# Moving the low halves of the expert weights between VectorE's and GpSimd's queues, three more shared results kept aside, and raw weights loaded by SyncE, in a one-core transformer block

## The reference

```python
h = layernorm(x) * (1 + ca) + sa
x = x + ga * (window_attention(h) @ w_out.T)          # 16 heads, window 64
h = layernorm(x) * (1 + cb) + sb
# router: 16 experts, the best 4 for each row, with weights w
y = sum over e of coeff[:, e] * ((silu(h @ Wg[e].T) * (h @ Wu[e].T)) @ Wd[e].T)   # inner width 176
z = (silu(h @ Sg.T) * (h @ Su.T)) @ Sd.T              # shared expert, inner width 352
x = x + gb * (y + z)
```

## Time and profile before

| | |
|---|---|
| span of the profiled execution | 556.1 us |
| its time on the device | 557.91 us |
| mean granted clock of TensorE | 0.969 of full speed |
| TensorE busy | 503.4 us (91%) |
| VectorE busy | 380.4 us (68%) |
| ScalarE busy | 281.0 us (51%) |
| GpSimd busy | 301.1 us (54%) |
| chain that ended last | PE 65%, DVE 15%, issue 7%, DMA 6%, POOL 4%, ACT 2% |

### The profile page before, as it was taken

How to read it: one execution, slowest core, us unless ns; L and a number is a source line. 1 busy time by engine, 2 the same in 40 slices (tenths; PEclk the granted TensorE clock), 3 DMA queues, 4 the chain that set the end, 5 groups by cost and what they waited for, 6 DMA issues and landing times.

```text
span 556.1 us, 11906 instructions
## 1 busy us (share of the span) xinstructions
PE 503.4 (91%) x3457; PEld 462.8 (83%) x3457; DVE 380.4 (68%) x1051; ACT 281.0 (51%) x735; POOL 301.1 (54%) x261
## 2 busy tenths in 40 slices
PE   2699999999999998999878787899999999999966
PEld 0589998999898898989655576789999999999956
DVE  6769952545768678686777668977677677777443
ACT  2358764464445545444463446455556555564311
POOL 6546611010225464354657539987766676677671
PEclk9999999999899999999777899999999999999979
DMA  7556996689678485642367447557777886776586
GB/s 195 150 164 215 259 304 193 176 216 221 179 235 252 145 242 162 195 126 75 123 231 237 149 126 163 88 104 133 130 122 129 198 129 128 129 130 111 103 260 151
DMA packets 72499, 94.23 MB, mean 169 GB/s; under 512 B 9339, under 2 KB 61882, under 8 KB 72118
## 3 DMA queue, kind: packets, MB, share of 16 engines
q1 hardware_dynamic: 53368, 60.35, 40.2%
q0 software_dynamic: 16384, 27.32, 23.9%
q10 hardware_dynamic: 2686, 5.81, 3.5%
HBM read 57.27 MB, written 41.88 MB: 178 GB/s over the span
## 4 chain that ended last, share of the span: by engine, by line
PE 65%; DVE 15%; issue 7%; DMA 6%; POOL 4%; ACT 2%; SPq 0%; DVEq 0%; POOLq 0%; ACTq 0%
PE GU_e L108 12%; PE YP_e L108 11%; PE O L1402 8%; PE QB L108 5%; PE VB L108 4%; PE TB L1392 3%; PE SB L1380 3%; PE HT_e L1982 3%; PE XT_e L1972 3%; POOL acc L1846 2%; PE TB L1390 2%; DMA acc<-h,ids_st 2%; PE SB L1377 2%; DVE lo L194 2%; PE Y L1419 2%
## 5 line engine op out<-in xcount | busy, mean ns | idle before, releaser
L1846 POOL DMA_INDIRECT acc<-h,ids_st x59 | 93.4, 1583 | 38.4 <-DMA acc<-h,ids_st 15.0
L143 POOL DMA_INDIRECT xs_scr<-h,slot_u x64 | 63.0, 984 | 62.0 <-PE TB L1392 25.3
L108 PE MATMUL GU_e<-gu_hi,xT 128*128 x316 | 82.6, 343 | 1.5 <-DVE xT L1873 0.8
L108 PE MATMUL YP_e<-dn_hi,aT 88*128 x316 | 67.6, 306 | 6.0 <-DVE aT L1878 6.0
L1772 ACT ACTIVATE aT<-HT_e 88x256 fp32r<-88x256 f32 (+1 forms) x89 | 34.9, 394 | 69.1 <-PE HT_e L1982 69.1
L949 ACT ACTIVATE prob<-TB 128x512 f32<-128x512 f32 x64 | 38.2, 597 | 58.2 <-PE TB L1392 57.4
L1402 PE MATMUL O<-raw,prob 128*128 128x99 f32 x512 | 67.1, 278 | 0.0
L1402 PEld LDWEIGHTS O<-raw,prob 128*128 128x128 f32 x512 | 62.4, 194 | 0.1
L1885 DVE TENSOR_TENSOR h_act<-GU_e,g_act 128x176 f32<-128x176 f32 (+1 forms) x89 | 32.0, 360 | 43.5 <-ACT g_act L1765 42.5
L108 PEld LDWEIGHTS YP_e<-dn_hi,aT 88*128 88x128 f32 x316 | 47.8, 188 | 13.0 <-issue 9.3
L108 PEld LDWEIGHTS GU_e<-gu_hi,xT 128*128 128x128 f32 x316 | 51.1, 189 | 2.1 <-issue 2.0
(11 more groups left out here) (245 smaller groups left out, 1221.9 us busy)
## 6 DMA issues: line engine op xcount, KB each, us to landing
x_st<-xs_scr SPq DMA_DIRECT2D x79, 144.0 KB
dn_hi<-k_scr SPq DMA_DIRECT2D x48, 192.0 KB, 3.9
k_scr<-raw SPq DMA_DIRECT2D x8, 768.0 KB, 6.1
dn_hi<-q_scr SPq DMA_DIRECT2D x24, 256.0 KB, 4.4
q_scr<-raw SPq DMA_DIRECT2D x8, 512.0 KB, 3.6
raw<-in_egu SPq DMA_DIRECT2D x8, 352.0 KB
raw<-in_x SPq DMA_DIRECT2D x16, 128.0 KB, 3.9
x_res<-in_x SPq DMA_DIRECT2D x32, 64.0 KB, 3.3
```

The source lines that it names most:

```text
L108: mm = eng.matmul(out, a, b, start=(i + j == 0), stop=(i == len(pairs) - 1 and j == 2))
L143: eng.indirect_dma_start(T["xs_scr"], bass.IndirectOffsetOnAxis(ap=T["slot_u"][:, par, t % 2, k:k + 1], axis=0), T["h2"][:, row, :], None) ...
L1846: eng.indirect_dma_start(acc, bass.IndirectOffsetOnAxis(ap=ids_st[:, r:r + 1].bitcast(U32), axis=0), results(r % 8), None, compute_op=ALU. ...
```

## The change

It moves `gu_low` 0 and 1 ahead of the last `residual`, and 2 to 5 behind them in the tail, each at an earlier place than before; VectorE makes six there, not five, and the ten others in steps 3 to 14 of the loop (eleven in steps 0 to 13 before). GpSimd makes 13 `dn_low` ahead of its first scatter, not five, and the last three behind scatters 8, 10 and 12 (one behind each of scatters 0 to 10 before). SyncE loads the raw weights of experts 13 to 15 and of the shared expert, not GpSimd, in its own loop of row loads, and waits ahead of that loop for what GpSimd waited for. Six shared results are kept aside, not three, and added in two operations in the last two tiles. The order of the stores follows that.

```diff
-HI_AHEAD, LO_AHEAD, DN_AHEAD = 13, 5, 5
+HI_AHEAD, LO_AHEAD, DN_AHEAD = 13, 6, 13
-LOW_STEPS = (0, 1, 3, 4, 5, 7, 8, 9, 11, 12, 13)
+LOW_STEPS = (3, 4, 5, 7, 8, 9, 11, 12, 13, 14)
...
         route_scores(PAIRS - 2)
+        gu_low(eng, T, 0)
+        gu_low(eng, T, 1)
         residual(LAST, 3, im, PAIRS - 1)
...
         steps_of_experts()
-        gu_low(eng, T, 0)
+        gu_low(eng, T, 2)
         tail_gate(2)
         steps_table()
+        gu_low(eng, T, 3)
         tail_out(0)
-        gu_low(eng, T, 1)
         tail_gate(3)
+        gu_low(eng, T, 4)
         table_out()
-        gu_low(eng, T, 2)
+        gu_low(eng, T, 5)
         tail_out(1)
         tail_gate(4)
-        gu_low(eng, T, 3)
         tail_out(2)
         tail_gate(5)
         tail_out(3)
-        gu_low(eng, T, 4)
         tail_out(4)
...
-    KEPT = 3
+    KEPT = 6
...
+        eng.wait_ge(ty_mm, NB)
+        eng.wait_ge(z_keep, 8 * NB)
+
         def step(s, r, i, first, last):
+            if s < NE - HI_AHEAD:
+                load_raw(eng, A, T, HI_AHEAD + s, HI_AHEAD + s + 1, w_last[s])
+            if s == NS - 40:
+                eng.dma_start(sgu_raw[:, :, :, :], A["sgu"]).then_inc(sgu_ld, 16)
+                eng.dma_start(sdn_raw[:, :, :], A["sd"]).then_inc(sdn_ld, 16)
             if runs(s, 0, NS - 5):
                 load_x(s + 4, r % 4)
...
-        eng.wait_ge(final, 2)
+        eng.wait_ge(final, 1)
+        store_out(0)
         store_out(1)
-        store_out(0)
-        eng.wait_ge(final, 3)
-        store_out(2)
         eng.wait_ge(fold, 3)
         store_out(5)
+        for k, g in enumerate((3, 2)):
+            eng.wait_ge(final, k + 2)
+            store_out(g)
         eng.wait_ge(fold, 4)
         store_out(6)
         store_out(7)
-        for g in (3, 4):
-            eng.wait_ge(final, g + 1)
-            store_out(g)
+        eng.wait_ge(final, 4)
+        store_out(4)
...
-            if s < NE - DN_AHEAD:
-                dn_low(DN_AHEAD + s)
-            if s in (1, 2):
-                load_raw(eng, A, T, HI_AHEAD + s, HI_AHEAD + s + 1, w_last[s])
+            if s in (8, 10, 12):
+                dn_low(HI_AHEAD + s // 2 - 4)
...
-            if n == 6:
-                add_kept()
+            if n == 8:
+                add_kept(0, 4)
+            if n == 9:
+                add_kept(4, 6)
```

More of the change, by code:

```diff
@@ L1833, in _ @@
             dn_low(e)
[L1834 to L1837, removed]
         eng.wait_ge(T["zeroed"], 16 * 9)
@@ L1847, in step @@
                                    None, compute_op=ALU.add).then_inc(sent[s % 2], 16)
-            if s < NE - DN_AHEAD:
-                dn_low(DN_AHEAD + s)
-            if s in (1, 2):
-                load_raw(eng, A, T, HI_AHEAD + s, HI_AHEAD + s + 1, w_last[s])
-            if s == NS - 40:
-                eng.dma_start(sgu_raw[:, :, :, :], A["sgu"]).then_inc(sgu_ld, 16)
-                eng.dma_start(sdn_raw[:, :, :], A["sd"]).then_inc(sdn_ld, 16)
+            if s in (8, 10, 12):
+                dn_low(HI_AHEAD + s // 2 - 4)
         for_steps(eng, step, NS)
@@ L1906, in add_late, with add_kept @@
             done.then_inc(final if n % 2 else z_late, 1)
-        def add_kept():
+        def add_kept(low, high):
             eng.wait_ge(z_late, KEPT)
-            eng.wait_ge(fold, 1)
-            eng.tensor_tensor(to_add[:, 0:KEPT, :], to_add[:, 0:KEPT, :], z_kept[:, 0:KEPT, :], ALU.add).then_inc(final, 1)
+            eng.wait_ge(fold, (high - 1) // 4 + 1)
+            eng.tensor_tensor(to_add[:, low:high, :], to_add[:, low:high, :], z_kept[:, low:high, :], ALU.add).then_inc(final, 1)
         x_lo(0, 0)
@@ L2109, in program @@
             T["odd_sums"] = last_use.enter_context(nc.sbuf_tensor("odd_sums", [P, TILES, D], F32))
-            T["z_kept"] = last_use.enter_context(nc.sbuf_tensor("z_kept", [P, 4, D], F32))
+            T["z_kept"] = last_use.enter_context(nc.sbuf_tensor("z_kept", [P, 6, D], F32))
         with ExitStack() as early:
```

## The result

Twenty runs of the change have a median of 562.74 us (559.4 to 569.3), twenty of the kernel before 561.51 us (547.6 to 570.3): 0.2% by the medians. The ratios with an interval leave out each kernel's slow runs. Here the ratio is 1.0172 [1.0133, 1.0211], but it sets a mean of 561.9 us for the change against some 552 us (561.9 / 1.0172) for the kernel before, 9 us under its median, so it leans on few runs there. In a second comparison (experiment 8), over six and eleven runs, it is 563.94 against 558.95 us, 1.0094 [1.0060, 1.0128]. So the change is slower, by about 1%; that it is more than that is not shown. The profiled execution took 563.65 us (span 561.7, mean granted clock 0.946) against 557.91.

The account below looks back on a forecast made before the run. Bounds: early expert steps and tail by gu_low held beside GpSimd's dn_low, later steps by TensorE, the end by folds, add and stores. 1.6 - 4.2 + 2.5 - 6.4 + 8.2 + 0.5 - 2.1 = +0.1: 564.2 us, range 555 to 571.

Parts of the forecast that it names:

- Four `gu_low` come a step too late: +8.2: Expert steps 12 to 15: TensorE waits 2.06 us in each for a gu_low made last in VectorE's step; +8.2 us.
- the clock set aside as a rival: Steps 12 to 15: TensorE's clock falls in the four waits, 7.6 us more, giving 571.8 us; chance 0.12.
- Raw weights on SyncE, +2.5: Early expert steps: rows of step 4 wait behind raw weights on SyncE's queue, so XT of step 2 waits; +2.5 us.
- upper end of 3.1: XT of step 2: its wait for rows behind the raw weights was put at 3.1 us at most.
- 1.9 + 2.9: Rows of step 4: 1.9 us for the raw weights plus 2.9 from the rows' issue to use, at the latest.
- No holds in the loop, -6.4: Expert steps: VectorE's gu_low no longer stand still beside GpSimd's dn_low; 6.7 us less 0.3 of another wait, -6.4.
- 4.6 forecast there: The part of the 6.4 us gained from holds that fell up to GU 11; 1.8 fell behind it.
- The tail, +1.6 and -4.2: Tail: two gu_low ahead of the last residual cost +1.6 us; no hold by GpSimd's run gains 4.2.
- Shared weights, +0.5: Shared expert's weights on SyncE, ahead of rows loaded four steps ahead: +0.5 us, between 0 and 1.5.
- the end, -2.1: End: 16 stores back to back behind VectorE's add, to 551.8 instead of 553.85 us; -2.1, between -6 and +1.
- The sum: All terms together: +0.1 us, so 564.2 us against a median of 564.14, no change.

Follow-up runs that it names:

- experiment 8: The change once more, no edit, profiled a second time: 563.94 us, beside 558.95 for the kernel before.
- experiment 2: The change with eight unused products at the end of TensorE's steps 11 to 14: 559.57 us, beside 565.48 for the kernel before.
- experiment 6: The change with gu_low in steps 3 to 9 and 11 to 13, raw weights behind the rows of SyncE's steps 2, 4, 6: 545.58 us, ratio to before 0.9771.
- experiment 9: The kernel before once more, no edit, for a second profile: 559.15 us.
- experiment 12: experiment 6 with the tail's gu_low 5 moved behind the fifth gate product, beside GpSimd's run of dn_low: 565.62 us, beside 545.46 for experiment 10.
- experiment 10: experiment 6 with the two gu_low ahead of the last residual put ahead of the last route_scores: 545.46 us, ratio to the kernel before 0.9698.
- experiment 7: The kernel before with only the change's end (six results kept, two adds, new store order): 556.35 us beside 558.95, ratio 0.9877.
- experiment 11: experiment 10 with the folds in tile-group order 4, 2, 1, 3 and four tiles stored from the first fold on: 545.38 us beside 545.46.
- experiment 3: The change with SyncE loading rows ahead of the raw weights, its wait behind the first row load: 564.55 us, beside 565.48 for the kernel before.
- experiment 5: The change with gu_low in steps 3 to 9 and 11 to 13, raw weights of experts 13 to 15 on GpSimd's queue: 553.8 us, beside 563.94 for the change.
- experiment 4: The change with gu_low in steps 3 to 9 and 11 to 13, and SyncE's rows ahead of the raw weights: 553.45 us.

## Why the prediction was wrong

**The step that failed: "Four `gu_low` come a step too late: +8.2", with the clock set aside as a rival at 0.12.** Place and mechanism of the waits were right (GU 12 to 15, last in VectorE's step, none at `a_lo`), and their size nearly: 6.7 us by experiment 2, steps of 4.2 us at full clock where 4.4 stood. But the argument against the clock's fall, that waits of up to 1.3 us had left it at 1.00, was carried over to waits of some 2 us, which measured 1.81 to 2.53. The clock fell behind the first of the four (the second, in the other profile) and cost 5.1 us. The rival's 7.6 was too much, its mechanism was what happened; the term is 11.8 us where 8.2 stood.

**Raw weights on SyncE, +2.5.** The wait was 3.57 us (2.93, 3.18 and 3.95 in three other profiles with the same order), above the upper end of 3.1. From the first raw weights' issue to that XT it took 6.0 us (320.44 to 326.43) where the bound had 1.9 + 2.9: the rows left SyncE 1.6 us later and took 4.41 us, not 2.9. Behind it step 3 ran at the lower clock, which the sum left out: from GU 3 to GU 7 the change takes 10.4 us, experiment 6, which has no wait there, 9.2. With the 3.5 us by which GU 3 is later than before, the term is about 4.7; against experiment 6, wait and burst together cost 5.8.

**No holds in the loop, -6.4.** Right in sign and place. Between GU 3 and GU 11 the kernel before takes 23.5 us and experiment 6 19.4; these 4.1 answer to the 4.6 forecast there. But the profile read was a lucky one behind GU 11 (experiment 9).

**The tail, +1.6 and -4.2.** Forecast -2.6, measured -4.3 and -2.5 in the two profiles. No hold is left, and experiment 12 shows what one costs. The +1.6 for two `gu_low` ahead of the `residual` was 0.7 to 1.2 (experiment 10).

**Shared weights, +0.5**, and **the end, -2.1**: +0.5 and -2.8, the latter confirmed alone (experiment 7, -3.9). The +0.5 agrees by luck: in the first profile step 16 still runs at the lower clock (2.99 us, 2.31 in the other three), and without these 0.7 us the stretch is 0.1 us longer than before.

**The sum.** +4.2 us by the means of two profiles each, +5.5 against the one profile that it was made against, where +0.1 stood. The loop (GU 0 to S 0) has it: +12.6 in that pair where +4.8 stood, while tail and end came out 2.3 better than forecast. That the median of 562.74 lies close to the forecast of 564.2 is no merit: the forecast rested on a median of 564.14 from three runs, and the twenty, these three among them, gave 561.51.

**What is better than both.** Experiments 6, 10 and 11 take 545.4 to 545.6 us: 2.3 to 3.1% under the kernel before by their ratios, and some 3% under the change. The idea of the change was sound; what it lost lay in one table of ten numbers and in the place of three loads and of the wait ahead of them.

## What to carry to other kernels

A wait that repeats is not only its own length: ask whether TensorE's clock stays up behind it, and take as safe only waits as short and as rare as those that the trace shows at full clock. When a list of deadlines is shortened, write beside each entry the step that needs it: four entries one step late cost 11.8 us here. And a large load ahead of small ones that are needed soon is judged by the lead of those small ones, and so is a wait that stands ahead of them on their queue: with the wait and the loads behind the rows of three steps, and the loads two steps apart, TensorE waited for no rows.

## What was not expected of the hardware

- A subtraction of VectorE with both operands in SBUF, 0.88 us alone, took 16.64 us beside a run of 13 operations of GpSimd with 1.22 us each. The Trainium skill's page "SBUF — State Buffer" (section "SBUF: two separate sides") tells of ports that the two engines share as an exclusive lock, held for the whole instruction of whichever starts first. The standstill agrees with it; that it lasts over 13 instructions, not to the end of the first, is more than the page says. Nor do the trace's times bear out that the first to start wins: in experiment 9 VectorE began 0.39 us ahead and was held.
- The granted clock fell to 0.50 with waits of 1.81 to 2.53 us in steps of 5 us, and stayed at 1.00 with waits of 1.1 to 1.3 us in steps of 3.5 us in the kernel before. Length alone does not decide: single waits of 1.73, 1.77 and 2.15 us (experiments 3, 5 and 4) left it at 1.00, while in experiment 7 a wait of 1.59 us behind others of 1.1 to 1.2 us was followed by 0.50, and one of 1.61 us in experiment 9 by 1.00. What decides was not tried.
- Where the 9 us of scatter ahead of the tail come from stays open; no run here changed that part.
